# A three-stage attention kernel: the second stage's first rounds issued within the first stage's last three, on shared memory

## The reference

```python
# first: x [128,128,256], ctx as keys and values
scores = jnp.einsum('bhdl,bhdm->bhlm', qh, kh) / sqrt(8) - 1e9 * mask
att = softmax(scores);  o = jnp.einsum('bhlm,bhdm->blhd', att, vh)
y = layernorm(o + x_t) * gamma + beta
# then the decoder layer
attn1 = mha(x, x, x, look_ahead_mask, ...);      out1 = layernorm(x + attn1)
attn2 = mha(ctx, ctx, out1, padding_mask, ...);  out2 = layernorm(out1 + attn2)
ffn = relu(out2 @ w1 + b1) @ w2 + b2;            out = layernorm(out2 + ffn)
```

## Time and profile before

| | |
|---|---|
| median of 3 runs | 4401.99 us (4399.11 to 4402.87) |
| the profiled execution | 4393.49 us |
| its span, first to last instruction | 4391.7 us |
| mean granted TensorE clock | 0.989 |
| TensorE matmul / weight load busy | 4098.9 us (93%) / 3365.3 us (77%) |
| VectorE busy | 3555.6 us (81%) |
| ScalarE busy | 3132.4 us (71%) |
| GpSimd busy | 2890.5 us (66%) |

### The profile page before, as it was taken

The page is one execution under the profiler, slowest core; times in us unless marked ns, Lnnn a source line. Parts: engine busy times, 40 slices in busy tenths (PEclk is TensorE's granted clock), DMA queues, the critical chain, the costliest instruction groups (busy, mean ns, idle before and its releaser), DMA issues. The chain is left out here.

```text
span 4391.7 us, 129316 instructions
## 1 busy us (share of the span) xinstructions
PE 4098.9 (93%) x46152; PEld 3365.3 (77%) x46152; DVE 3555.6 (81%) x13895; ACT 3132.4 (71%) x6279; POOL 2890.5 (66%) x4576
## 2 busy tenths in 40 slices
PE   7999999999999979999999987999999997999999
PEld 5777777777777757777777766888888876999998
DVE  7999999999999969999999985787787885555555
ACT  5777777777777758888888875777777775545453
POOL 4777777777777747777777765777777762444444
PEclk8999999999999989999999999999999999999999
DMA  5444444444444456666666656778888862122221
GB/s 134 125 125 121 126 122 124 125 123 127 120 126 124 118 109 155 173 161 174 161 173 169 165 139 163 195 197 203 194 197 204 192 173 97 66 72 73 73 73 53
DMA packets 813639, 608.75 MB, mean 139 GB/s; under 512 B 61592, under 2 KB 751304, under 8 KB 813000
## 3 DMA queue, kind: packets, MB, share of 16 engines
q1 hardware_dynamic: 800952, 594.90, 51.6%
q10 hardware_dynamic: 12048, 5.58, 0.6%
HBM read 175.66 MB, written 117.54 MB: 67 GB/s over the span
## 5 line engine op out<-in xcount | busy, mean ns | idle before, releaser
L1207 DVE CUSTOM_DVE_ANT_0 l_junk<-bank,mask 128x256 bf16<-128x256 f32 x2048 | 775.5, 416 | 36.5 <-PE bank L878 21.0
L1048 ACT ACTIVATE mha_probs<-bank 128x512 f32<-128x512 f32 x1024 | 603.7, 600 | 265.9 <-DVE bank L1222 146.5
L1048 ACT ACTIVATE l_probs<-bank 128x512 f32<-128x512 f32 x1024 | 600.7, 593 | 159.5 <-DVE bank L1222 148.6
L1222 DVE TENSOR_TENSOR bank<-bank,mask0t 128x512 f32<-128x512 f32 x832 | 572.2, 688 | 5.5 <-PE bank L910 3.1
L1207 DVE CUSTOM_DVE_ANT_0 mha_junk<-bank,mask 128x128 bf16<-128x128 f32 x2048 | 462.0, 284 | 31.6 <-PE bank L878 31.4
L878 PE MATMUL bank<-mha_stack 96*128 96x128 bf16 (+1 forms) x4096 | 364.5, 220 | 79.3 <-DVE mha_max_parts L1207 47.8
L1630 ACT ACTIVATE ffn_hidden<-ffn_h,ffn_b_s 128x512 f32<-128x512 f32 x256 | 176.6, 690 | 353.0 <-PE ffn_h L1576 342.3
L910 PE MATMUL bank<-mha_stack 99*128 99x128 bf16 (+1 forms) x4096 | 396.6, 220 | 16.7 <-DMA mha_stack<-mha_max_rows 11.9
L910 PE MATMUL bank<-l_stack 99*128 99x128 bf16 x4096 | 402.1, 220 | 7.5 <-ACT l_probs L1048 3.4
L878 PE MATMUL bank<-l_stack 96*128 96x256 bf16 x2048 | 374.9, 274 | 31.6 <-DVE l_max_parts L1207 24.9
L1222 DVE TENSOR_TENSOR bank<-bank,mask1t 128x512 f32<-128x512 f32 x512 | 354.4, 693 | 61.5 <-PE bank L910 58.5
(11 more groups left out here) (198 smaller groups left out, 11375.1 us busy)
## 6 DMA issues: line engine op xcount, KB each, us to landing
mha_stack<-mha_parts SPq DMA_DIRECT2D x1530, 128.0 KB, 3.2
l_stack<-l_parts SPq DMA_DIRECT2D x1024, 64.0 KB
l_stack<-l_parts SPq DMA_DIRECT2D x256, 128.0 KB
rows_o<-mha_resid SPq DMA_DIRECT2D x64, 512.0 KB, 3.3
cols_o<-mha_y_t SPq DMA_DIRECT2D x64, 512.0 KB, 2.9
l_x_pad<-in_x SPq DMA_DIRECT2D x64, 256.0 KB, 3.4
l_c_pad<-in_ctx SPq DMA_DIRECT2D x64, 256.0 KB, 3.1
l_resid<-in_x_t SPq DMA_DIRECT2D x64, 256.0 KB, 3.1
```

The costliest lines, as they stand in the source:

```text
L1048: nc.scalar.activation(probs[:, i % RING, :], tbank[i % 2][:, :], ACT.Exp).then_inc(att_exp, 1)
L1207: ins = nc.vector.tensor_tensor_reduce(out=junk[:, i % 2, cols], in0=sbank[i % 2][:, cols], in1=mask, scale=1.0, scalar=LOWEST, op0=ALU.ad ...
L1222: nc.vector.tensor_tensor(bank_, bank_, mask.unsqueeze(1).to_broadcast([P, 4, P]), ALU.add).then_inc(att_masked, 1)
```

## The change

Rounds -3, -2 and -1 of the second stage are issued within rounds 62, 63 and 64 of the first (`overlap=3`), without the shift by three slots, and the second block starts at round 0.

For that, part of the second stage's memory must exist while the first stage runs. A new group of tiles, `kept`, holds a stack, values, `parts1`, `junk`, `units_row`, `max_parts` and `max_rows`. The first stage uses all of it; its two stacks of 16 rows of heads are the two halves of the one kept stack, and both its `parts` lie in `parts1`. In the second and third stages the kept stack and values are those of even units. The stack and values of odd units are allocated when the first stage has ended, as before.

New waits keep the second stage from overwriting what the first still reads:

- the fills of unit 0's stack and its row of ones wait for the first stage's last attention product (`att_mm`);
- unit 0's values wait for the first stage's last value product; unit 1's projections for its last fills; unit 0's first maxima row for its last maxima DMA; VectorE's maxima for its last transposes of maxima;
- unit 0's first score product waits for the first stage's outputs in the banks it uses. In the tail the first stage's output transposes use bank `tbank[0]` and the bias products `tbank[1]`.

Unit 1's fills (24, and its row of ones), and the load of unit 0's residual, are issued in round 0, after the barrier. GpSimd's clearing of 52 semaphores moves there too, the second half of the values gets its column of ones there, and the residual's bias is added in slot 7 of round 0 and not in slot 3. VectorE's settings of PSUM, values and `units_row` at the second stage's start are gone.

The diff, cut (left out: the same indexing change `stack[:, u.par, ...]` to `stack[u.par][:, ...]` in `score_step`, `attend_step`, `pv_tile`, `value_out` and `max_rows_out`, and the counts that the new waits use):

```diff
+    c["kept"] = {n: sb_mid(f"kept_{n}", shape, dt) for n, shape, dt in (
+        ("stack", [P, 32, TOK], BF16), ("vals", [P, 64, D + 1], F32), ("parts1", [P, 4, 3, TOK], BF16),
+        ("junk", [P, 2, 512], BF16), ("units_row", [3, 1, TOK], BF16), ("max_parts", [P, TILES * 3 * 16], F32),
+        ("max_rows", [48, 2 * P], BF16))}
...
+    kept = c["kept"]
+    parts = [kept["parts1"][:, 0:2, :, :], kept["parts1"][:, 2:4, :, :]] if conv else [
+        sb("parts0", [P, HALVES, 3, TOK], BF16), kept["parts1"]]
+    max_rows = kept["max_rows"][0:3 * H, :]
+    max_parts = kept["max_parts"][:, 0:TILES * 3 * H].rearrange("p (j a h) -> p j a h", j=TILES, a=3)
+    junk = kept["junk"]
+    if conv:
+        stack = [kept["stack"][:, 0:16, :], kept["stack"][:, 16:32, :]]
+        by_unit = kept["vals"][:, :, :].rearrange("p (u j h) d -> p u j h d", u=2, j=TILES)
+        vals = [by_unit[:, 0, :, :, :], by_unit[:, 1, :, :, :]]
+    else:
+        stack = [kept["stack"][:, :, :]]
+        vals = [kept["vals"][:, :, :].rearrange("p (j h) d -> p j h d", j=TILES)]
+    units_row = own("units_row", [3, 2, P], BF16) if phase == 2 else kept["units_row"][:, :, 0:TOK if conv else P]
...
+        if not conv:
+            stack.append(sb("stack1", [P, 2 * H, TOK], BF16)[:, :, :])
+            vals.append(sb("vals1", [P, TILES, H, D + 1])[:, :, :, :])
...
+        if phase == 1 and u.number() == 0:
+            eng.wait_ge(stage0["att_mm"], c["stage0_attends"])
...
-            sp.wait_ge(row_ready, 2 if phase == 2 else 1)
+            if phase == 1 and 0 in halves:
+                sp.wait_ge(stage0["row_ready"], 1)
+                sp.wait_ge(stage0["att_mm"], c["stage0_attends"])
+            elif phase != 1:
+                sp.wait_ge(row_ready, 2 if phase == 2 else 1)
...
-            if phase == 2 and t.number() == 0:
+            if phase == 1 and t.number() == 0:
+                load_resid(t)
+            if not conv and t.number() == 0:
                 fill_stack(t.plus(1), 0)
             if exists(t.plus(1), N) and t.number() != -1:
                 fill_stack(t.plus(1), 1)
-            if phase == 1 and t.number() == -1:
-                fill_side(sp, t.plus(1), 0, 0)
-                fill_stack(t.plus(1), 1)
-                fill_ones(0, 1)
+            if phase == 1 and t.number() == 0:
+                fill_ones(1)
             if phase != 1 and t.number() == -2:
...
-            if phase != 1 and t.number() == -2:
+            if phase == 1 and t.number() == -2:
+                fill_side(sp, t.plus(2), 0, 0)
+                fill_stack(t.plus(2), 1)
+                fill_ones(0)
+            elif t.number() == -2:
                 for side in range(2) if phase == 2 else (1,):
                     for half in range(2):
                         fill_side(sp, t.plus(2), half, side)
-            elif exists(t.plus(2), N) and t.number() != -2 and (phase != 2 or t.number() != -1):
+            elif exists(t.plus(2), N) and (conv or t.number() != -1):
                 fill_stack(t.plus(2), 0)
-            if not conv and exists(t.plus(1), N):
+            if not conv and exists(t.plus(1), N) and (phase == 2 or t.number() != -1):
                 load_resid(t.plus(1))
...
+            if i == 0 and phase == 1 and u.number() == 0:
+                pe.wait_ge(stage0["work_out"], c["stage0_before_last"])
...
+            if i == 0 and phase == 1 and u.number() == 1:
+                for p in range(2):
+                    for half in range(2):
+                        act.wait_ge(stage0[f"stack_in{p}{half}"], c["stage0_fills"])
...
-            if phase == 1 and t.number() == -1:
-                fill_side(act, t.plus(1), 0, 1)
-                round_x(t.plus(2))
...
-                if slot == SPLIT_SLOT and exists(t.plus(3), N) and (phase != 1 or t.number() != -2):
+                if slot == SPLIT_SLOT and exists(t.plus(3), N):
                     round_x(t.plus(3))
                 yield
+            if phase == 1 and t.number() == -2:
+                fill_side(act, t.plus(2), 0, 1)
...
-            if phase != 2:
+            if phase == 1:
+                return
...
-            if phase == 1 and t.number() == -1:
+            if phase == 1 and t.number() == 0:
                 for s in c["signals"][0].values():
                     pool.sem_clear(s)
-                rest_of_x(t.plus(2))
             for slot in range(16):
-                if phase == 1 and slot == plan["bias_slot"] and exists(t, N):
+                if phase == 1 and slot == (7 if t.number() == 0 else plan["bias_slot"]) and exists(t, N):
...
-                run(nc, first, ahead=second, overlap=2, lag=3)
+                run(nc, first, ahead=second, overlap=3, ahead_starts=True)
             second["allocate"]()
             third = attention(nc, top, mid, c, io, 2)
-            run(nc, second, before=1, ahead=third, overlap=3, ahead_starts=True)
+            run(nc, second, before=0, started=True, ahead=third, overlap=3, ahead_starts=True)
```

74 lines of the change are left out of this document (40 added, 34 removed).

## The result

The changed kernel took 4409.53 us (median of 12 runs, 4405.71 to 4414.80); the kernel before, in the same session, 4401.12 (12 runs, 4396.40 to 4407.80). The ratio is 1.0019, 95% interval 1.0012 to 1.0027: slower by some 8.4 us, 5 to 12 by the interval. That is real, and just inside the 0.2% that the prediction called no change. The profiled execution took 4408.86 with a span of 4407.1.

The account below looks back on a forecast made before the run. VectorE nearly fills full rounds but is half idle or worse in rounds 64 and -1, some 50 us. Terms -3.8 + 2.0 + 3.0 + 3.0 = +4.2 us on 4393.49, plus 8.5 to the median: 4406; range 4393 to 4418.

Parts of the forecast that it names:

- Round 63 grows by 15.0: First stage's round 63, taking in unit 0's four projections, goes from 17.1 to 32 us; growth range 2.7 to 16.4.
- The relative of the earlier trace: Second stage's last attention round, carrying the third stage's projections: 41.7 us against 32.1; gives round 63 a growth of 16.4.
- Fills: -3.8: Unit 0's fills no longer wait for the barrier, so its first score product comes 3.8 us earlier, at 1604.1.
- ScalarE's six come after its rounding: ScalarE's six fills of unit 0 follow its rounding of unit 1's input, at 1593.6 against SP's 1590.9.
- The rival that counted 10.5 from SP's start: Unit 0's first score comes 10.5 us after SP's first fill, at 1601.4, a gain of 6.4; 4403; chance 0.08.
- The tail 2.0: First stage's tail, now inside round -1, adds TensorE's eight bias products to its path: 2.0 us, ends 0 and 5.
- the barrier 3.0: Barrier now before round 0, where attention waits for GpSimd's subtraction for unit 2: 3.0 us, ends 0.4 and 3.5.
- Unit 1's fills: 3.0: Round 0: fills issued behind the barrier make TensorE wait at unit 1's scores: 3.0 us, ends 0 and 4.1.
- The clock rival: TensorE's clock falls below about 0.7 in round 63, costing 8 us, 4414; chance 0.20 together with held fills.
- Only-the-work: Rival: round 63 grows only by VectorE's added work, 2.7 us, staying under 24; 4394 or 4386; chance 0.17.
- The overlap was there: Rival denied overlap: round -1 starts at 1597 as before, only costs remain, +8, 4410; within the slower case's 0.20.
- its own trap: Round 63: VectorE's splitting steps between mask additions wait for ScalarE's copies, holding the next exponential; 3.12 us, four times.

Follow-up runs that it names:

- e2: Changed kernel with unit 0's splits kept on VectorE, each one slot later; round 63's last exponential came 25.30 us after its first, where it was 33.98.
- e4: Changed kernel with six of unit 1's first 12 fills issued from ScalarE's queue instead of SP's; 4408.54 us.
- e10: Changed kernel with all 24 fills of unit 0 issued by SP, none by ScalarE; ratio 1.0020 to the kernel before.
- e1: Changed kernel with unit 0's splits in round 63 given to GpSimd, ScalarE and GpSimd instead of VectorE; ratio 0.9992 to the kernel before.
- e7: Changed kernel with unit 1's first 12 fills on two queues and SP's 12 for the second half held until those have landed; 4407.54 us.
- e9: Changed kernel with round 63's splits off VectorE and all 24 fills of unit 0 issued by SP; ratio 0.9981 to the kernel before.
- e3: Changed kernel with 72 unused TensorE products in slots 7 to 15 of round 63; passage 3.0 us shorter, no gain in the timed runs.

## Why the prediction was right, and where not

The forecast was no change, +4.2 us on the passage, 4406; measured were +7.4 on the passage and 4409.5. The direction and the build of it were right: what overlap takes out comes back as a slow round 63 and two waits in round 0. By its terms:

- **Round 63 grows by 15.0.** It grew by 17.5. The mechanism was right, splits in front of masks, four times; e2 shows it without touching the work. The number was built as a sum of durations (3.12 per projection). The row that measures it is VectorE's 13.2 us of waiting, 2.0 to 4.3 each; beside it stands VectorE's own work for the four splits. The relative of the earlier trace rows gave 16.4, the nearer value.
- **Fills: -3.8.** It was -2.6, with round 63's further 2.5 in it. SP's began within 0.1 us of the end of the last attention products (1593.06 + 0.63), as told. The step that failed is "ScalarE's six come after its rounding", 2.7 later: they began 0.8 after SP's, ahead of the rounding. From SP's start to the first score it took 11.85 us, not 10.5. The rival that counted 10.5 from SP's start erred on that number alone. By the Trainium skill, DMA: Bandwidth & Descriptors, section "Issuing engines are not separate DMA queues", issuing from several engines can save issue time only, since the transfers run on the same 16 DMA engines. The trace agrees that two queues brought no more bytes, but here not even the issue time was saved: 12.7 us against 11.2 (e4 against the changed kernel) and 11.85 against 9.98 (the changed kernel against e10) for two queues against one.
- **The tail 2.0 and the barrier 3.0.** Together 4.2 less 0.3. The tail's part is 1.6 (10.19 less 8.57), and it is what the prediction named, the bias products, 1.73 us of TensorE. The barrier's part is 2.6 (3.49 less 0.85), less the 0.3. It was put down to GpSimd's subtraction, which does end last; but VectorE's maxima end 0.9 before it, so without it the barrier still costs some 1.7. The prediction did not see ScalarE's issuing in the tail. In the changed kernel the fills' own landing covers it: TensorE waits for them behind it, 1.77 us. In e1 nothing covers it.
- **Unit 1's fills: 3.0.** This is the term that was mis-sized. The wait is 4.19, its high end, and round 0 grew by 6.4. The clock row accounts for the other 2.2: 4.79 us of products at 1.2 GHz behind the wait, where before the clock was full. The prediction priced the stop and not the slow products after it. No run takes the slow clock away alone; over the runs round 0 grew by 1.2 (e7) to 3.4 us (e9) more than this wait.

The clock rival, 8 us in round 63 if the clock were below 0.7 and a third at 0.83, met a clock of 0.82; its third is 2.7, near the 2.5 by which the growth was short, but e3 puts at most 1.1 there. Only-the-work (growth 2.7) did not come, and e1, with the splits off VectorE, still grew by 7.9: no run here came near it. The overlap was there, and full rounds kept their length.

The errors partly cancelled (first score 1.2 later than told, tail and barrier 1.1 cheaper, round 0 3.4 dearer): the sum was 3 us short of a true +7.4, which lies close to the 8.8 that split the forecast from "slower". That the time stayed under that line was in part luck. What the prediction didn't see is that its own trap was cheap to leave: one slot of delay (e2) shortens round 63 by 8.7, more than the whole growth of the passage.

## What to carry to other kernels

When a step that waits for two other engines is put into an in-order queue, look at what stands right behind it; a slot of delay for it (e2) was worth 8.7 us here, and taking its work away only 0.9 more. Price a stop of TensorE with the slower products that follow it. And count the issue of DMAs on a computing engine as that engine's time: 0.7 to 1.1 us for each fill here, and look at what stands behind it in that engine's program.
